# Routing in f16 pairs of tiles, and expert biases added by VectorE, in a tokeniser, linear attention and mixture-of-experts kernel

## The reference

```python
h = tok(x)                    # 16 x 255 patches of 16 x 64 values: norm, product with W (1024 x 256), bias
h = h + attn(layernorm(h))    # 8 heads, linear recurrence over the 255 tokens
h = h + ffn(layernorm(h))

def ffn(x):                                       # x: 4080 tokens x 256
    logits = (x @ w_red) @ normalised(wg).T       # 8 experts
    gates = softmax(logits)
    scores, idx = max(gates), argmax(gates)       # one expert for each token
    h = gelu(x @ W1[idx] + b1[idx])               # 256 -> 512
    return (h @ W2[idx] + b2[idx]) * scores       # 512 -> 256
```

## Time and profile before

| | |
|---|---|
| median of 3 runs | 633.92 us (631.78 to 635.15) |
| the profiled execution | 633.04 us |
| its span, first to last instruction | 631.0 us |
| TensorE, VectorE, ScalarE, GpSimd busy | 88%, 69%, 36%, 33% |
| mean granted TensorE clock | 0.951 of full speed |
| tokenising and mixing | to about 421 us |
| routing, to the first up product | 421 to 455.5 us |
| slots | to the end |

### The profile page before, as it was taken

The page is one execution under the profiler, slowest core; times in us unless marked ns, Lnnn a source line. Parts: engine busy times, 40 slices in busy tenths (PEclk is TensorE's granted clock), DMA queues, the critical chain, the costliest instruction groups (busy, mean ns, idle before and its releaser), DMA issues. The chain is left out here.

```text
span 631.0 us, 12973 instructions
## 1 busy us (share of the span) xinstructions
PE 553.3 (88%) x3517; PEld 374.2 (59%) x3518; DVE 438.4 (69%) x1128; ACT 227.3 (36%) x436; POOL 207.4 (33%) x284
## 2 busy tenths in 40 slices
PE   3988999999999999998669999961489999999992
PEld 2866666666677777774337676740246656666661
DVE  2768888888888888986649999978534444444441
ACT  1425555444554445555311111120033333333330
POOL 4463222222222222222011222324415555555531
PEclk9989999999999999999979999995679999999997
DMA  9211222221122221100113333210102222211210
GB/s 255 76 35 35 67 67 67 67 67 53 47 66 67 67 67 67 50 18 33 33 47 105 108 113 105 93 60 1 38 18 63 68 63 65 61 58 60 64 39 0
DMA packets 32424, 39.92 MB, mean 63 GB/s; under 512 B 7203, under 2 KB 23844, under 8 KB 32401
## 3 DMA queue, kind: packets, MB, share of 16 engines
q1 hardware_dynamic: 22348, 25.01, 12.7%
q0 software_dynamic: 3744, 9.34, 5.1%
q10 hardware_dynamic: 6308, 5.28, 2.9%
HBM read 30.92 MB, written 9.59 MB: 64 GB/s over the span
## 5 line engine op out<-in xcount | busy, mean ns | idle before, releaser
L494 PE MATMUL banks<-proj,xnT_h 128*128 128x512 f16 x384 | 114.7, 381 | 1.7 <-DVE early L1149 1.7
L475 PE MATMUL banks<-early 128*128 128x256 f16 x768 | 88.5, 276 | 2.6 <-DVE wo_l L974 2.4
L475 PEld LDWEIGHTS banks<-early 128*128 128x128 f16 x768 | 75.9, 99 | 12.4 <-DVE wo_l L974 2.6
L494 PE MATMUL banks<-proj,xnT_l 128*128 128x512 f16 x192 | 73.0, 380 | 0.0
L1541 DVE TENSOR_TENSOR vo<-banks,vo 128x256 f16<-128x256 f32 x39 | 16.6, 426 | 70.8 <-ACT vo L921 70.8
L1733 POOL DMA_INDIRECT out<-proj,vo x39 | 39.5, 1013 | 79.6 <-DVE vo L1558 79.6
L921 ACT ACTIVATE vo<-banks 128x256 f16<-128x256 f32 x39 | 14.9, 383 | 126.8 <-PE banks L663 126.8
L494 PEld LDWEIGHTS banks<-proj,xnT_h 128*128 128x128 f16 x384 | 37.7, 98 | 38.0 <-DVE early L1149 2.0
L696 PE MATMUL banks<-w2h,vo 128*128 x312 | 57.5, 273 | 1.2 <-DVE proj L1556 1.2
L676 PE MATMUL banks<-w1h,vo 128*128 x156 | 55.1, 394 | 3.1 <-ACT vo L927 2.1
L1658 POOL TENSOR_TENSOR w1l<-stage,w1h 128x512 f32 (+1 forms) x16 | 18.5, 1158 | 102.9 <-ACT w1h L815 102.9
(11 more groups left out here) (258 smaller groups left out, 1272.3 us busy)
## 6 DMA issues: line engine op xcount, KB each, us to landing
early<-in_x SPq DMA_DIRECT2D x16, 512.0 KB, 3.4
stage<-in_W SPq DMA_DIRECT2D x32, 256.0 KB, 2.8
early<-lam_by_chunk SPq DMA_DIRECT2D x32, 132.0 KB
token_rows<-rows ACTq DMA_DIRECT2D x16, 129.0 KB, 2.4
token_rows<-rows ACTq DMA_DIRECT2D x16, 112.9 KB, 2.1
vo<-in_tok_W ACTq DMA_DIRECT2D x2, 512.0 KB, 7.2
early<-lam_by_head SPq DMA_DIRECT2D x16, 64.0 KB
vo<-token_rows,vo POOLq DMA_INDIRECT x39, 2.9
```

The costliest lines, as they stand in the source:

```text
L475: last = mm(bank(2 + j, D), x_[:, k, at:at + P], w[:, KG * half + k, :], start=(half == 0 and k == 0 and x_ is gT_h and w is wtok_h), stop ...
L494: last = mm(dst, a, c, start=(i == 0), stop=(i == n - 1))
```

## The change

- **Pairs of tiles.** `in_slot`, `carried` and `at_place` are laid out as pair of tiles x slot (or place) x tile of the pair, so that the innermost run of every operand is two f16 values side by side (`slot_twice`, `place_twice` hold each number twice).
- **Three carried values.** The id less 2040 is one f16 value (`ids16`), so there is one id product in place of two. All are made by VectorE; GpSimd has no part in the routing.
- **Counts.** `oh` is f16, padding is taken out before it, and `not_before` holds -1 for tokens that do not lie ahead, so that the product plus `cum` is the rank. The number of slots of an expert comes from rounding. The maximum is taken of unscaled logits, before the roots are there.
- **Unread products** (`keep_busy`, 128x512): 14 ahead of the counts, 28 behind them, 14 behind the gathering products.
- **Biases.** `b1` and `b2` are loaded to all partitions into the space of `rows` (2.1 MB and 1.0 MB) at the end of SyncE's program. The bias products leave TensorE. VectorE adds `b1` to the up product into `pre` (`add_bias`), which ScalarE's GELU now reads, and adds `b2` times the score to the row of the token (`scaled_bias`). VectorE loads the number of the expert for each slot. The splitting of the biases in the prologue and `pick_expert` are gone.

The core of the diff (waits of the routing steps on each other left out):

```diff
-        in_slot = early[:, 4096:4096 + TILES * SLOTS // 2].bitcast(F16).rearrange("p (t i) -> p t i", t=TILES)
...
+        in_slot = early[:, 4096:4096 + TILES * SLOTS // 2].bitcast(F16).rearrange("p (g i t) -> p g i t", g=B, t=2)
+        carried = early[:, 1536:1536 + 3 * TILES * SLOTS // 2].bitcast(F16).rearrange("p (g v i t) -> p g v i t",
+                                                                                     g=B, v=3, t=2)
...
+        found = banks[:, 5, 0:3 * SLOTS].rearrange("p (v i) -> p v i", v=3)
...
+        b1_wide = flat_rows[:, 0:E * FF].rearrange("p (e f) -> p e f", e=E)
+        b2_wide = flat_rows[:, E * FF:E * (FF + D)].rearrange("p (e d) -> p e d", e=E)
+        pre = flat_rows[:, E * (FF + D):E * (FF + D) + 2 * FF].rearrange("p (w f) -> p w f", w=2)
...
+            sp_.wait_ge(s["table_in"], 16 * 3 * B)
+            sp_.wait_ge(s["r_args"], 1)
+            sp_.dma_start(b1_wide.rearrange("p e f -> p (e f)"), b1.rearrange("e f -> (e f)").partition_broadcast(P)
+                          ).then_inc(s["biases_in"], 16)
...
+            keep_busy(14)
             pe.wait_ge(s["oh_ready"], 1)
             ohf = oh.rearrange("p t e -> p (t e)")
-            mm(bank(0, 256), before[:], ohf, start=True, stop=True)
-            mm(bank(1, 256), ones[:], ohf, start=True, stop=True).then_inc(s["counts"], 1)
-            pe.wait_ge(s["ids_ready"], 1)
+            mm(bank(1, 256), count_rows[:, 1, :], ohf, start=True, stop=True).then_inc(s["counts"], 1)
+            mm(bank(0, 256), count_rows[:, 0, :], ohf, start=True, stop=True).then_inc(s["counts"], 1)
+            keep_busy(28)
+            pe.wait_ge(s["carried_ready"], 3)
             for q in range(4):
                 pe.wait_ge(s["places_ready"], q + 1)
                 for t in range(8 * q, 8 * q + 8):
-                    last = mm(banks[:, 5, 0:4 * SLOTS], at_place[:, t, :], carried[:, t, :, :].rearrange("p v i -> p (v i)"),
+                    last = mm(banks[:, 5, 0:3 * SLOTS], at_place[:, t // 2, :, t % 2],
+                              carried[:, t // 2, :, :, t % 2].rearrange("p v i -> p (v i)"),
                               start=(t == 0), stop=(t == TILES - 1))
             last.then_inc(s["found_ready"], 1)
+            keep_busy(14)
...
-                    pe.wait_ge(s["gelu_done"], i)
+                    pe.wait_ge(s["pre_done"], i)
                 for c in range(DC):
                     for x_, w in ((xh, w1h), (xh, w1l), (xl, w1h)):
-                        mm(bank(0), x_[:, c, :], w[:, bass.ds(e * DC + c, 1), :].rearrange("p a b -> p (a b)"),
-                           start=(c == 0 and w is w1h and x_ is xh), stop=False)
-                mm(bank(0), pick_expert[:, bass.ds(e, 1), :].rearrange("p a b -> p (a b)"), bias_hl[:, 0:FF],
-                   start=False, stop=True).then_inc(s["m1_ready"], 1)
+                        last = mm(bank(0), x_[:, c, :], w[:, bass.ds(e * DC + c, 1), :].rearrange("p a b -> p (a b)"),
+                                  start=(c == 0 and w is w1h and x_ is xh), stop=(c == DC - 1 and x_ is xl))
+                last.then_inc(s["m1_ready"], 1)
...
-                mm(bank(3, D), pick_expert[:, bass.ds(e, 1), :].rearrange("p a b -> p (a b)"), bias_hl[:, FF:FF + D],
-                   start=False, stop=True).then_inc(s["m2_ready"], 1)
+                        last = mm(bank(3, D), a[:, w, f, :], w_[:, bass.ds(e * FC + f, 1), :].rearrange("p a b -> p (a b)"),
+                                  start=(f == 0 and w_ is w2h and a is gh), stop=(f == FC - 1 and a is gl))
+                last.then_inc(s["m2_ready"], 1)
...
-                af(gel, bank(0), ACT.Gelu).then_inc(s["gelu_done"], 1)
+                af(gel, pre[:, w, :], ACT.Gelu).then_inc(s["gelu_done"], 1)
...
+            dve.wait_ge(s["h2_done"], TILES)
+            raw_lg = rows[:, :, ROWC:ROWT]
+            r.step(reduce(mx, raw_lg, AX, ALU.max))
...
+            r.step(tt(oh, raw_lg, wide(mx, T8), ALU.is_ge))
+            r.step(tt(oh, oh, repeated(rank_w16[:], T8), ALU.mult))
+            r.step(reduce(mw, oh, AX, ALU.max))
+            r.step(tt(mw, mw, valid[:], ALU.mult))
+            tt(oh, repeated(rank_w16[:], T8), wide(mw, T8), ALU.is_equal).then_inc(s["oh_ready"], 1)
+            r.step(tt(lg, raw_lg, wide(mx, T8), ALU.subtract))
+            tt(lg, lg, rows[:, :, 1:2].to_broadcast(T8), ALU.mult).then_inc(s["r_args"], 1)
+            tot = bank(1, TILES * E).rearrange("p (t e) -> p t e", e=E)
+            r.step(ts(tiles8, cum[:, TILES - 1, :], 1.0 / P, (P - 1) / (2 * P), ALU.mult, ALU.add))
+            dve.wait_ge(s["counts"], 2)
+            r.step(tt(t8.rearrange("p t e -> p (t e)"), bank(0, TILES * E), cum.rearrange("p t e -> p (t e)"), ALU.add))
...
+            r.step(ts(padded[:, 1:E + 1], magic8, ROUND, float(P), ALU.subtract, ALU.mult))
+            r.step(scan(starts, padded, zeros[:, 0:E + 1], 0.0, ALU.add, ALU.add))
...
+            r.step(tt(in_slot, by_pairs(slot_of).unsqueeze(2).to_broadcast(TS),
+                      slot_twice[:].unsqueeze(1).to_broadcast(TS), ALU.is_equal))
+            dve.wait_ge(s["r_exp"], 1)
+            r.step(reduce(sumexp, lg, AX, ALU.add))
+            tt(carried[:, :, 0], in_slot, by_pairs(ids16[:]).unsqueeze(2).to_broadcast(TS),
+               ALU.mult).then_inc(s["carried_ready"], 1)
...
+            r.step(tt(score, score, valid[:], ALU.mult))
...
+                tt(carried[:, :, 1 + h], in_slot, by_pairs(score_parts[:, h]).unsqueeze(2).to_broadcast(TS),
+                   ALU.mult).then_inc(s["carried_ready"], 1)
+                four = slice(4 * q, 4 * q + 4)
...
+                tt(at_place[:, four], by_pairs(place_of)[:, four].unsqueeze(2).to_broadcast(TP),
+                   place_twice[:].unsqueeze(1).to_broadcast(TP), ALU.is_equal).then_inc(s["places_ready"], 1)
...
+            ts(gather_id, found[:, 0], float(ID_MIDDLE), None, ALU.add).then_inc(s["route_ready"], 1)
...
+            def expert_of(i):
+                return dve.value_load(sloti[0:1, bass.ds(i, 1)], min_val=0, max_val=E - 1)
+            def add_bias(i, w, e):
+                dve.wait_ge(s["m1_ready"], i + 1)
...
+                tt(pre[:, w, :], bank(0), b1_wide[:, bass.ds(e, 1), :].rearrange("p a b -> p (a b)"),
+                   ALU.add).then_inc(s["pre_done"], 1)
+            def scaled_bias(i, w, e):
+                row = xr[:, w, 2:ROWC]
+                stt(row, b2_wide[:, bass.ds(e, 1), :].rearrange("p a b -> p (a b)"), slot_score[:, bass.ds(i, 1)], row,
+                    ALU.mult, ALU.add).then_inc(s["z_done"], 1)
             def finish(i, w, g):
 
                 dve.wait_ge(s["m2_ready"], i + 1)
+                dve.wait_ge(s["z_done"], i + 1)
...
+                    e = expert_of(i)
+                    add_bias(i, w % 2, e)
                     if not (last and w == count - 1):
                         split_rows(i + 1)
                     if not (last and w >= count - 2):
                         norm_rows(i + 2, (w + 2) % RING, g if w + 2 < RING else g + 1)
+                    scaled_bias(i, w, e)
...
-            TS = [P, TILES, SLOTS]
-            pool.wait_ge(s["in_slot_ready"], 1)
-            ptt(carried[:, :, 0, :], in_slot, id_parts[:, 0].unsqueeze(2).to_broadcast(TS), ALU.mult)
-            ptt(carried[:, :, 1, :], in_slot, id_parts[:, 1].unsqueeze(2).to_broadcast(TS), ALU.mult).then_inc(s["ids_ready"], 1)
```

More of the change, by code:

```diff
@@ L69 @@
 OUT_OF_RANGE = 1 << 20
+ID_MIDDLE = B * NTOK // 2
 ROUND = 1.5 * 2 ** 23
@@ L222, in build @@
         mx, mw, sumexp, posf = (rt[:, 32 * i:32 * i + 32] for i in range(4))
-        r8 = over(8 * 4)
-        ntile, tend, tstart, _ = (r8[:, 8 * i:8 * i + 8] for i in range(4))
+        tiles8, magic8 = over(8), over(8)
+        padded = over(10)[:, 0:E + 1]
+        starts = over(10)[:, 0:E + 1]
         slotf = over(SLOTS)
@@ L341, in _ @@
             sp_.dma_start(alpha_bias[:], W_ab.partition_broadcast(P)).then_inc(s["misc_in"], 16)
-            for half in range(2):
-                two = slice(E * half, E * half + E)
-                sp_.dma_start(bias_in[two, 0:FF], b1).then_inc(s["bias_in"], 16)
-                sp_.dma_start(bias_in[two, FF:FF + D], b2).then_inc(s["bias_in"], 16)
             load_x(1)
@@ L1480, in _ @@
             r.settle()
-            r.step(tt(posf, posf, pad_pos[:], ALU.add))
-            r.settle()
             r.step(ts(posd, posf, 1.0 / P, -(P - 1) / (2 * P), ALU.mult, ALU.add))
@@ L1500, in _ @@
             for q in range(4):
-                eight = slice(8 * q, 8 * q + 8)
-                tt(at_place[:, eight], wide(place_of[:, eight], [P, 8, P]), repeated(place[:], [P, 8, P]),
-                   ALU.is_equal).then_inc(s["places_ready"], 1)
+                four = slice(4 * q, 4 * q + 4)
+                TP = [P, 4, P, 2]
+                tt(at_place[:, four], by_pairs(place_of)[:, four].unsqueeze(2).to_broadcast(TP),
```

(1 more changed line is left out.)

183 lines of the change are left out of this document (72 added, 111 removed).

## The result

The changed kernel takes **607.34 us** (median of 4 runs, 606.33 to 607.95) against 634.53 for the kernel before in the same series (4 runs, 631.78 to 637.57): ratio 0.9583, 95% interval 0.9548 to 0.9618. Faster, by 27 us. The forecast was worked out from the profiled execution of the kernel before (633.04 us): 32.0 less, 601.0. The profiled execution of the change took 607.44 us (605.6 of it the span), 25.6 less, so 6.4 us of the forecast gain did not come. Ratios are of undisturbed executions; in the series of *unroll_both*, *ring8_unroll* and *ring8_unroll_all*, two of seven executions of the kernel before took 975 and 1976 us and are left out of them.

What follows compares the result with a forecast made beforehand. The prediction took VectorE's dependent chain to bound the routing and TensorE, without gaps, the later slots. Routing 12.5, first slots 5.2, later slots 14.0 and drain 0.3 make 32.0 off 633.0: 601.0 us, range 592 to 618.

Steps and rivals of the forecast that it cites:

- The routing: Routing: VectorE's dependent chain gets shorter, the gather index ready at 436.5 us against 449.00, −12.5 us.
- rival (c): Routing masks: pairs of tiles do not double VectorE's rate; 606 us; chance 0.08.
- First slots: Slots 0 to 2: TensorE's clock taken as held, 9.1 us for 14.14; with the lead-in −5.2 us.
- rival (d): Before slot 0: unread products do not hold TensorE's clock until that slot; 603 to 606 us; chance 0.10.
- The bias tables: Before slot 0: 3.1 MB on SyncE's queue at 255 GB/s, 12.3 us, hidden until the bias addition at 444.5.
- Rival (e): Before slot 0: bias tables load at the lower rate, 108 GB/s, until 453.5; 610 us; chance 0.05.
- The ring: Later slots, six rows: 5.1 us from copy to landing plus 1.9 to 2.1 of work; period at least 3.5 to 3.6.
- Rival (b): Later slots: the ring closes faster, landings at 2.6 or so; period 3.42, 593 us; chance 0.15.
- the 3.65: Later slots: period in us, ring plus register work; 35 further slots × 0.40 = −14.0 us.
- The register load of VectorE: Each slot: VectorE's added register load taken as under 0.5 us and hidden; bounds 0 and 1.3.
- (a): Later slots: VectorE binds, 3.06 us plus an unhidden load; at 1.0 the period is 4.06, 615 us; chance 0.17.
- (f): Every slot: register load with arithmetic costs VectorE 1.6 us or more; slower than before, 636 us; chance 0.03.

Runs made afterwards that it cites:

- unroll_both: The changed kernel with TensorE's and VectorE's slot loops written out, six rows kept in the ring: 603.31 us, ratio 0.9516 to the kernel before.
- ring8_unroll: The changed kernel with a ring of eight rows and TensorE's and VectorE's slot loops written out: 592.24 us, ratio 0.9342 to the kernel before.
- ring8_unroll_all: The changed kernel with eight rows, TensorE's, VectorE's and GpSimd's loops written out, and unread products of 44 and 30: 591.71 us, ratio 0.9333 to the kernel before.
- unpaired: The changed kernel with routing masks kept tile by tile in f16, one value repeated along the innermost index: 607.88 us, ratio 0.961 to the kernel before.
- ring8: The changed kernel with a ring of 8 rows instead of 6: 598.59 us, ratio 0.9445 to the kernel before.
- banks: The changed kernel with down products alternating between two PSUM banks, TensorE waiting for the finish of the slot two before: 606.49 us, ratio 0.9572 to the kernel before.
- old_bias: The changed kernel's routing, but biases by TensorE's products as before, without bias tables or VectorE additions: 617.94 us, ratio 0.9743 to the kernel before.
- unroll: The changed kernel with only TensorE's slot loop written out, six rows kept: 602.29 us, ratio 0.9523 to the kernel before.
- regload: The changed kernel with VectorE reading the expert's number twice in each slot: 610.28 us, ratio 0.9643 to the kernel before.
- more_fill: The changed kernel with 44 and 30 unread products in place of 28 and 14 ahead of the first slot: 605.43 us, ratio 0.955 to the kernel before.
- nobusy: The changed kernel with all three groups of unread products (14, 28 and 14) left out: 605.8 us, ratio 0.9566 to the kernel before.

## Why the forecast held, and where it failed

**The routing: right.** Forecast −12.5. From the statistics to the index took 16.2 us (422.61 to 438.77), against 15.4 forecast and 27.9 before, so it gave 11.7 of the 12.5. Masks of 0.80 and 0.68 are the lower bound that was taken (0.81, 0.69), and *unpaired* puts the old 1.45 and 1.22 beside them, so rival (c) falls by its mechanism. The rule of the Trainium skill ("Vector Engine (DVE) Microarchitecture Reference", section 5.1), of which the trace of before showed one half, holds here in both. The failing part is small: "the 32 gathering products ... end in time for the index either way". They began 0.83 us behind the first place mask's start, ran mostly at the low clock (0.54) for 3.31 us where 3.0 had been reckoned, and the index waited 0.62 for them.

**First slots: the wrong step is "the clock stood longer than that after the last product, so I take it as held".** The last unread product ended at 441.62, the transposes came at 443.61, and the clock did stand over that gap; but the windows show 0.96 and then 0.50 from about 445 on, within slot 0. Slots 0 to 2 took 11.4 us for 9.1. That is what rival (d) forecast, though not for its reason: the clock had fallen ahead of the gathering products, but it came back during the fourteen unread ones. What differs between the runs is how long TensorE then stood idle. First transposes in *ring8* and in *banks*, with what TensorE waited ahead of them:

```profile
441.87 0.41 PE L672 MATMUL banks<-ident,vo 128*128 128x128 f32 x2 [2.01 <-DVE vo L1533]
```

```profile
443.22 0.41 PE L672 MATMUL banks<-ident,vo 128*128 128x128 f32 x2 [0.61 <-DVE vo L1533]
```

In the change and in *ring8*, *old_bias*, *unroll*, *unroll_both* and *ring8_unroll* the wait was 1.99 to 2.08 us, and the clock fell about when slot 0 began. In *banks*, *regload* and *unpaired* the fourteen products began at the low clock, so they lasted 4.2 to 4.6 us instead of 3.2 to 3.3; the wait was 0.61 to 1.10, and the clock stood at 1.00 through slot 2. *more_fill* takes the wait away altogether. The time at stake, 1.3 to 2.5 us, is as small as the spread of one kernel.

**The bias tables: right.** The first of the two loads was in after 7.7 us, and all had landed before 435, at 328 to 492 GB/s in whole microseconds from 427 to 434, faster than the 255 that was taken. Rival (e) had nothing for it.

**The ring: right, and it is what the sum rested on.** From the copy's end to the normalisation 0.90 + 1.32 + 2.96 = 5.18 us (forecast 5.1), with 1.88 of work behind it: two slots hold 7.06, 3.53 each (forecast 3.5 to 3.6). *ring8* takes it away and gains 6.5 us in the slots. Rival (b), a period of 3.42, is excluded.

**The turn: left out of the sum.** Of the six slots of a turn (four full turns after the first) two pairs are held by the ring (7.0 to 7.2 us from copy to copy, nearly always with a wait for the row), and the third pair takes 8.0 to 8.2 with no such wait: that is TensorE's turn, some 1.0 us on top of the ring. The forecast said "TensorE makes such a load each slot". It makes 51 for 39 slots, and a branch; hidden before by a period of 4.05 and a queue that ran ahead, as *old_bias* shows. The trace of before had the count and the 303 ns, and the forecast drew on neither. With six rows, writing out TensorE's loop gave back 2.7 us in the slots; with eight, writing out TensorE's and VectorE's gave 5.6. Which part of the turn costs how much (the branch and the way back to the loop's first instructions, the arithmetic, the three reads) no run tells apart. Theory (A), that the ring exposed it, falls with *banks* and *ring8*: the long slots stayed. What exposed it is the shorter period itself, by *old_bias* against *ring8*. In the last turn the rows came later, 3.7 us and more behind the load's start for 3.0, and in the other versions with six rows and short slots as well; why is open.

So the 3.65 came out as near as it did (3.715, and 0.065 × 35 = 2.3 us) by some luck. Its ring part measured 3.53; the 0.05 to 0.15 beyond that stood for "register work" and had no row behind it, and what filled it, with 0.18, was a turn that the forecast had not thought of. Nor did line 1540 come every 3.65 us: five slots of a turn took 3.3 to 3.7 and one 5.1 to 5.3, over the 4.0 that was named as a sign of being wrong. The period was right as a mean only.

**The register load of VectorE: the size was right, the margin smaller than stated.** 0.31 is under the 0.5 that was taken as hidden, and rivals (a) and (f) needed 1.0 and 1.6. But *regload* shows that 0.3 more is not hidden at all: VectorE's steps fill the 3.3 us of an ordinary slot of the change. (Rival (a)'s own cycle of 3.06 does not come out of the earlier trace rows: 2.16 of work and the two additions' 0.61 and 0.39 are 3.16. Only the chance of (a) hangs on it.) The note beside it, the Trainium skill's 200 ns per register loaded from HBM ("Runtime: NRT & Kernel Launch", "Instruction fetch mechanics"), is of another source; from SBUF the rows show 0.30.

**TensorE's floor:** forecast 3.34, measured 3.26 in *ring8_unroll*. **GpSimd's contention:** line 1562, with two inputs in SBUF, lasted 0.47 to 0.52, about as long as line 1571 with its one input in PSUM (0.47 to 0.49), while GpSimd's loads took 1.10 and its stores 1.02: no drag that shows. **Drain:** 19.12 us for 19.59, forecast −0.3.

In sum +1.5 (before the routing) + 0.8 + 2.3 + 2.3 − 0.2 − 0.2 (what lies around the span, 1.84 us instead of 2.04) is +6.4 us. Of that 2.3 is the clock in the first slots, 2.3 the turn in the later ones, and nearly a quarter stood there before the routing began.

## What to carry to other kernels

When a stage's period shrinks, list what the old period hid once per loop turn, not only once per slot: register reads, the branch, values read again at the top of the body. Count the instructions of a queue against the number of slots (51 for 39 said it here, in the trace of the kernel before) and look whether the queue runs ahead of its engine. A ring's length is cheap to size from three rows (store's start, load's start, landing) plus the work between; do that before shortening the stage, and give the ring what the new period needs (here eight rows for six, 6.5 us in the slots). With eight rows and the loops of TensorE and VectorE written out, this kernel runs at 592 us, 15 under the change and 42 under the kernel before.

## What the runs showed of the hardware

- A two-operand VectorE step all in f16 on 1248 elements took 0.80 us with two elements side by side in each innermost run, and 1.45 with one value repeated; on 1024 elements 0.68 and 1.22.
- TensorE's granted clock follows its work late: in *nobusy* it was 0.50 until 436.0, over nearly all of the gathering products (433.11 to 436.30), 1.00 in the window 436.50 to 438.00, when the engine had nothing to do, and 0.50 again in that of 439.50 to 441.00, with the first slot still to come.
- With fourteen unread products, in nine versions, the clock stood through slot 2 where TensorE had been idle for 0.61 to 1.10 us ahead of the first transposes, and fell about when slot 0 began where it had been idle for 1.99 to 2.08. At the end of the products it was at 1.00 in all nine.
- A register read from SBUF cost a sequencer 0.30 us on TensorE and 0.31 on VectorE, and at most 0.56.
- The first reduction of the routing moved between 420.4 and 422.5 us from one profiled execution to the next, over versions that are the same up to there.
